# Dividing a group's attention products once, by sums that a column of ones yields, instead of normalising every tile of probabilities

## The reference

```python
q, k, v = split(x @ Wq + bq), split(x @ Wk + bk), split(x @ Wv + bv)
attn = jnp.einsum('bhqd,bhkd->bhqk', q, k) / np.sqrt(8)
attn = jnp.where(causal, attn, -jnp.inf)
attn = jax.nn.softmax(attn, axis=-1)
y = jnp.einsum('bhqk,bhkd->bhqd', attn, v)
y = y.transpose(0, 2, 1, 3).reshape(b, s, e)
return y @ Wo + bo
```

## Time and profile before

| | |
|---|---|
| median of 3 runs | 4177.26 us (4172.37 to 4178.75) |
| the profiled execution | 4182.92 us |
| its span (first to last instruction) | 4181.1 us |
| stage 1 in it | 0 to 682 us |
| busy, whole span: PE, DVE, ACT, POOL | 93%, 79%, 74%, 62% |

### The profile page before, as it was taken

One profiled execution on the slowest core, in us unless ns is written; L12 is line 12 of the kernel. 1 busy time (PEld: TensorE's weight loads), 2 busy tenths in 40 slices (PEclk: granted clock), 3 DMA queues, 4 the chain that ended last, 5 costly groups with the idle time before them and its releaser, 6 DMA issues.

```text
span 4181.1 us, 190344 instructions
## 1 busy us (share of the span) xinstructions
PE 3900.5 (93%) x78816; PEld 3039.7 (73%) x78816; DVE 3305.5 (79%) x5294; ACT 3091.6 (74%) x10376; POOL 2581.2 (62%) x2583
## 2 busy tenths in 40 slices
PE   6888885999998999989999989999899999899998
PEld 3555554888866888848888668888488887588884
DVE  6778874988866888938888668989489886698894
ACT  5877785888865888838888658888488886588883
POOL 4667765766645676627666456766377664566660
PEclk9999998999999999999999999999999999999999
DMA  1000001111111111111111111111111111111110
GB/s 35 2 2 2 2 2 53 47 45 45 46 56 38 45 47 45 44 50 44 49 44 46 58 36 47 44 49 42 53 44 47 47 44 61 35 45 46 47 43 26
DMA packets 100195, 167.40 MB, mean 40 GB/s; under 512 B 26224, under 2 KB 33648, under 8 KB 99056
## 3 DMA queue, kind: packets, MB, share of 16 engines
q1 hardware_dynamic: 99312, 154.89, 12.6%
HBM read 26.13 MB, written 2.10 MB: 7 GB/s over the span
## 4 chain that ended last, share of the span: by engine, by line
PE 69%; issue 9%; POOL 3%; DVE 1%; ACT 0%; DMA 0%; SPq 0%; POOLq 0%; DVEq 0%; ACTq 0%
PE s_bank L1177 13%; PE s_bank L1246 10%; PE s_bank L1259 9%; PE s_bank L1198 8%; PE s_bank L1157 5%; PE s_proj L1222 4%; PE s_proj L1223 4%; PE s_proj L1224 4%; PE s_bank L1209 2%; PE s_bank L1210 2%; PE s_bank L1211 2%; PE s_bank L1167 2%; PE s_bank L1140 1%; POOL s_rotated L802 1%; PE s_bank L1289 1%
## 5 line engine op out<-in xcount | busy, mean ns | idle before, releaser
L802 POOL TENSOR_TENSOR s_rotated<-s_rotated,s_by_sin 128x512 f32<-128x512 f32 x768 | 983.8, 1302 | 227.3 <-DVE s_by_sin L1087 225.2
L811 POOL TENSOR_TENSOR s_probs<-s_probs,s_rden 128x256 f32<-128x256 f32 x768 | 479.7, 641 | 729.8 <-DVE s_rden L1027 729.3
L901 ACT ACTIVATE s_probs<-s_bank,s_neg_max 128x64 f32<-128x64 f32 x3072 | 908.0, 310 | 5.7 <-DVE s_neg_max L1020 5.6
L783 DVE TENSOR_TENSOR s_qk<-s_rotated,s_inv_norm 128x1024 f32<-128x1024 f32 x384 | 743.8, 1937 | 11.5
L1082 DVE TENSOR_TENSOR s_rotated<-s_proj,s_cos 128x1024 f32<-128x1024 f32 x384 | 469.6, 1223 | 241.5 <-ACT s_sq L935 240.9
L901 ACT ACTIVATION_READ_ACCUMULATOR s_probs<-s_bank,s_neg_max 128x1 f32 x3072 | 636.1, 207 | 0.0
L891 ACT ACTIVATE s_probs_t<-s_bank 64x512 f32<-64x512 f32 x384 | 226.8, 591 | 524.8 <-PE s_bank L1157 524.8
L1177 PE MATMUL s_bank<-s_qk 32*32 32x64 f32 x49152 | 581.4, 223 | 26.3 <-issue 25.9
L1177 PEld LDWEIGHTS s_bank<-s_qk 32*32 32x32 f32 x49152 | 510.9, 103 | 115.4 <-issue 114.6
L213 POOL TENSOR_TENSOR s_probs<-s_probs,s_rden 128x384 f32<-128x384 f32 (+3 forms) x512 | 406.4, 802 | 206.1 <-DVE s_rden L406 202.2
L824 POOL TENSOR_TENSOR s_sq<-s_sq 128x512 f32<-128x512 f32 x384 | 490.2, 1277 | 65.5 <-ACT s_sq L935 59.8
(11 more groups left out here) (118 smaller groups left out, 8156.2 us busy)
## 6 DMA issues: line engine op xcount, KB each, us to landing
s_v<-s_v SPq DMA_DIRECT2D x384, 192.0 KB, 2.5
s_v<-s_v SPq DMA_DIRECT2D x384, 64.0 KB, 2.4
s_qk<-f_wqk SPq DMA_DIRECT2D x6, 1024.0 KB, 6.4
s_xs_raw<-u SPq DMA_DIRECT2D x48, 128.0 KB
s_xf<-u SPq DMA_DIRECT2D x48, 128.0 KB, 2.3
s_xs_raw<-u SPq DMA_DIRECT2D x48, 127.8 KB
s_xf<-u SPq DMA_DIRECT2D x48, 127.8 KB, 2.6
s_qk<-f_wv SPq DMA_DIRECT2D x6, 512.0 KB, 6.8
```

The source lines that it names most:

```text
L783: return nc.vector.tensor_tensor(qk[:, quad % 2, :, :, at:at + TOKS], rotated[:, par, :, :, :], by, ALU.mult)
L802: nc.gpsimd.tensor_tensor(rotated[:, par, :, half, :], rotated[:, par, :, half, :], by_sin[:, :, 1 - half, :], (ALU.subtract, ALU.add)[half])\
L811: nc.gpsimd.tensor_tensor(part, part, by, ALU.mult).then_inc(S["probs_done"], 1)
L901: last = nc.scalar.activation(probs[:, par, h, b, :], score_bank[h][:, b * KEYS:(b + 1) * KEYS], ACT.Exp, scale=-1.0, bias=neg_max[:, par, ...
```

## The change

The probabilities are no longer normalised. The padded value matrix gets a bias of one in the ninth of each head's 32 columns, where weight and bias were zero; the product of a head's unnormalised probabilities with its values then holds the row sum in that row. When a group's four query blocks are done, ACT copies `y_bank` to `y_t` as before; a new product with a constant matrix `den_row` spreads each head's sum over its 32 partitions, back into `y_bank`; DVE takes the reciprocal of the whole bank (128 x 512) into `inv_den`; and POOL multiplies `y_t` by it. The per-unit reciprocal, the accumulator read and the per-unit multiplication on POOL are gone. The copy stands where it stood (+7), the new product is issued by PE at +8, the reciprocal by DVE at +9, the multiplication by POOL at +10. The next group's first value products (at +10) wait for the reciprocal in place of the copy, the output projection waits for the multiplication. The work at fixed unit numbers moves by three units. One constant more is loaded at the start.

```diff
-WO_AT, RES_LN_AT, X_LN_AT, PREP_AT = 9, 12, 18, 24
+WO_AT, RES_LN_AT, X_LN_AT, PREP_AT = 12, 15, 21, 27
+COPY_LAG, SPREAD_LAG, INVERT_LAG, DIVIDE_LAG = PV_LAG + 1, PV_LAG + 2, PV_LAG + 3, PV_LAG + 4
...
-                 (ident[:, :], d["c_ident"]), (causal[:, :], d["c_causal"]), (own_rows[:, :], d["c_own_rows"])]
+                 (ident[:, :], d["c_ident"]), (causal[:, :], d["c_causal"]), (own_rows[:, :], d["c_own_rows"]),
+                 (den_row[:, :], d["c_den_row"])]
...
+        def group(s, par, t, lag, first):
+            of = behind(s, par, t, lag, first)
+            return (of[0], of[2] // (QB * HPG)) if of and (of[2] + 1) % (QB * HPG) == 0 else None
...
-            def normalise(s, u):
-                n = P * (UNIT_LIST[u][1] + 1)
-                pool.wait_ge(S["rden_done"], s * UNITS + (u + 1))
-                row = probs[:, u % N_PROBS, 0:n]
-                nc.gpsimd.tensor_tensor(row, row, rden[:, u:u + 1].to_broadcast([P, n]), ALU.mult)\
-                  .then_inc(S["probs_done"], 1)
+            def divide(s, g):
+                pool.wait_ge(S["y_inv"], s * GROUPS + (g + 1))
+                nc.gpsimd.tensor_tensor(y_t[:, g, :], y_t[:, g, :], inv_den[:, :], ALU.mult).then_inc(S["y_done"], 1)
...
-                                         bias=neg_max[:, t:t + 1], accum_out=den[:, t:t + 1]).then_inc(S["exp_done"], 1)
+                                         bias=neg_max[:, t:t + 1]).then_inc(S["exp_done"], 1)
...
-                of = behind(s, par, t, 1, first)
+                of = group(s, par, t, INVERT_LAG, first)
                 if of:
-                    u = of[2]
-                    dve.wait_ge(S["exp_done"], of[0] * UNITS + (u + 1))
-                    nc.vector.reciprocal(rden[:, u:u + 1], den[:, u:u + 1]).then_inc(S["rden_done"], 1)
+                    n = of[0] * GROUPS + of[1]
+                    dve.wait_ge(S["y_spread"], n + 1)
+                    wait(dve, S["y_done"], n)
+                    nc.vector.reciprocal(inv_den[:, :], y_bank[:, :]).then_inc(S["y_inv"], 1)
...
             def output(s):
-                pe.wait_ge(S["y_ready"], s * GROUPS + GROUPS)
+                pe.wait_ge(S["y_done"], s * GROUPS + GROUPS)
...
-                    pe.wait_ge(S["probs_done"], us * UNITS + (u + 1))
+                    pe.wait_ge(S["exp_done"], us * UNITS + (u + 1))
...
                     if b == 0 and not (first and g == 0):
-                        pe.wait_ge(S["y_ready"], us * GROUPS + g)
+                        pe.wait_ge(S["y_inv"], us * GROUPS + g)
...
+                of = group(s, par, t, SPREAD_LAG, first)
+                if of:
+                    pe.wait_ge(S["y_ready"], of[0] * GROUPS + of[1] + 1)
+                    nc.tensor.matmul(y_bank[:, :], den_row[:, :], y_t[:, of[1], :], start=True, stop=True)\
+                      .then_inc(S["y_spread"], 1)
...
+        "c_den_row": ((np.arange(P)[:, None] % PADH == HD1)
+                      & (np.arange(P)[:, None] // PADH == np.arange(P)[None, :] // PADH)).astype(f32),
...
+    bv = pad_heads(i["L0_attn_bv"]).reshape(HEADS, PADH)
+    bv[:, HD1] = 1.0
```

More of the change, by code:

```diff
@@ L127, in build_stage1 @@
         neg_max = sb("s1_neg_max", [P, UNITS])
-        den = sb("s1_den", [P, UNITS])
-        rden = sb("s1_rden", [P, UNITS])
+        den_row = sb("s1_den_row", [P, P])
+        inv_den = sb("s1_inv_den", [P, SEQ])
         probs = sb("s1_probs", [P, N_PROBS, SEQ])
@@ L135, in build_stage1 @@
                  "q_split k_ready k_split "
-                 "v_ready diag_vector diag_pool score_done max_done exp_done rden_done probs_done tr_done pt_vector pt_scalar "
-                 "pv_done y_ready wo_done res_done").split()
+                 "v_ready diag_vector diag_pool score_done max_done exp_done tr_done pt_vector pt_scalar "
+                 "pv_done y_ready y_spread y_inv y_done wo_done res_done").split()
         S = {n: sem("s1_" + n) for n in names}
@@ L227, in unit @@
             def unit(s, par, t, first, last):
-                if t < UNITS:
-                    normalise(s, t)
+                of = group(s, par, t, DIVIDE_LAG, first)
+                if of:
+                    divide(*of)
                 if t < UNITS and not last:
@@ L295, in unit @@
                     nc.scalar.activation(probs[:, t % N_PROBS, 0:n], score_bank[t % 4][:, 0:n], ACT.Exp, scale=-1.0,
-                                         bias=neg_max[:, t:t + 1], accum_out=den[:, t:t + 1]).then_inc(S["exp_done"], 1)
[L297 to L301, removed]
+                                         bias=neg_max[:, t:t + 1]).then_inc(S["exp_done"], 1)
+                of = group(s, par, t, COPY_LAG, first)
+                if of:
+                    g = of[1]
+                    act.wait_ge(S["pv_done"], of[0] * SETS + (g + 1) * QB)
                     if g == 0 and not first:
@@ L1393, in lay_out @@
         "a_bk": four_times(np.asarray(i["L0_attn_bk"])[None]).reshape(GROUPS, P).T,
-        "a_bv": pad_heads(i["L0_attn_bv"]), "a_bo": np.asarray(i["L0_attn_bo"])[:, None],
+        "a_bv": bv.reshape(HEADS * PADH), "a_bo": np.asarray(i["L0_attn_bo"])[:, None],
         "f_wqk": qk_all.reshape(DEPTH, DIM, QUADS * 4 * P),
```

## The result

The changed kernel takes 4328.16 us (median of 4 runs, 4322.53 to 4332.34) against 4174.82 us: 1.0367 times the time before, 95% interval 1.0349 to 1.0385. It is slower, outside the range that was given, and 160 us above the forecast.

What follows compares the result with a forecast made beforehand. No engine full, four waiting for each other: 12.6 us of old waits against 11.0 us of new work and waits, 80.2 to 78.6 us a sequence; eight save 12.8, less 3.4 at the ends: 4168 us, range 4122 to 4224 (own 4145 to 4190).

Steps and rivals of the forecast that it cites:

- The reciprocal of 128x512 at 0.69 us: DVE's new reciprocal, four a sequence: 512 elements at 1.05 ns each, 2.4 us of DVE a sequence.
- second rival: DVE's reciprocal is slow and PE waits for the excess: 4211 us at 2.05 us, 4287 at 4.4; chance 0.20.
- The wait for it: PE's value products at +10 wait for DVE's reciprocal: 0.8 us each, 3.2 us a sequence.
- The old waits that go, 12.6 us: PE's waits at transposes, scores, projections and variance that vanish: 12.6 us a sequence, leaving 0.8 at transposes and scores.
- POOL's leg: Transposes waiting for POOL's normalised probabilities: by itself worth 1.3 to 8.1 us a sequence.
- The knot between DVE and ACT: Per-unit reciprocal stands before later maxima, so DVE can't run ahead of ACT; DVE's 6.1 us wait a sequence goes.
- The product 3.4 us and its wait 4.4 us: Spreading product on PE at +8, 0.86 us each, and its wait for ACT's copy of y, 1.1 us each.
- The wait for the inversion, 3.2 us: PE's value products at +10 wait 0.8 us for DVE's reciprocal; bounds nothing to 1.3 us each.
- The shift at nothing, -1 to +1 us: Fixed-place work moved three units later: no cost, bounds -1 to +1 us a sequence.
- The ends, 3.4 us: Once: one more load, 0.5 us, and the last group's product, reciprocal and POOL division, 2.9 us.
- The query copies near 0.47 us: Sign in the profile after: DVE's query copies, slow ones taken as beside POOL's work, gain 1.8 us a sequence.

Runs made afterwards that it cites:

- filler: Changed kernel with 12 useless bf16 products of 128x512 filling PE's wait for the reciprocal: 4334.30 us, ratio 1.0389.
- no_division: Kernel before without accumulator read, per-unit reciprocal and POOL's multiplication, nothing added or shifted: 4140.12 us, ratio 0.9915.
- shift_only: Kernel before without any division, with output projection, layer norms and projections three units later: 4155.54 us, ratio 0.9940.
- own_bank: Changed kernel with inversion as Exp(-Ln(x)) on ACT and the spreading product in its own bank, taken from the four score banks: 4218.71 us, ratio 1.0108.

## Why the prediction was wrong, by its own steps

- **The reciprocal of 128x512 at 0.69 us: wrong, and the main cause.** It takes 3.35 us. The text had the slow reciprocal as its second rival, with prices of 2.05 and 4.4 us, and chose against it by the equal minima of one and four elements. The minimum of several hundred short instructions is no price; the medians, at 3.7 ns an element, were nearer to the 6.25 ns, and the two prices of the rival, 2.05 and 4.4 us, enclose the 3.35 us. The page that the prediction cites from the Trainium skill ("VectorE: DVE Perf Modes", on the fixed hardware budget) speaks of a repeat count of 8. The runs show 6.25 ns an element, about six times the 1.05 ns of the reduction in the earlier trace rows: fewer than eight, far more than one. The estimate of 4.3 us from that page was nearer than the 0.69 us that was taken. The weight should have gone to the rival.
- **The wait for it: right in kind.** The value products wait 3.2 us, which is what the rival's mechanism says. What the rival lacked is the clock: by its terms 3.35 us is 4 x 2.66 = 10.6 us a sequence, and measured are 99.1 - 85.2 = 13.9. The 3.7 us that filler saved by keeping the clock up are about the difference.
- **The old waits that go, 12.6 us: three times too much.** Measured 4.4 us. The step that failed is the one from "DVE and ACT now lie some 15 us below PE's 74.9" to 0.8 us of waits left at transposes and scores: in no_division the two lie 18 us below the length of the sequence, and PE still waits 28.5 us in five sequences at the transposes alone, 5.7 each. It compared sums over a sequence, where the bound changes every few units.
- **POOL's leg, 1.3 to 8.1 us:** 2.5 us, in its range. The knot between DVE and ACT: 1.9 us.
- **The product 3.4 us and its wait 4.4 us:** the wait is 1.0 us each, nearly as said, but the two together lengthen a sequence by 3.6 us only. This error of 4.2 us went the other way and hid half of the 8.2 us by which the old waits were overestimated.
- **The wait for the inversion, 3.2 us:** 3.3 us, with 0.5 us a group seen at PE and POOL's division in it.
- **The shift at nothing, -1 to +1 us:** +2.5 us. Not in the bounds.
- **The ends, 3.4 us:** the last chain is longer, the reciprocal being 3.35 us, and the output projection behind it runs its first passes at the low clock (its eight passes take 5.70 us there against 3.70 in the earlier trace rows, the granted clock is 0.50 over the first 3.1 us of them). Stage 1 is 156.0 us longer (838.3 against 682.3), of which eight sequences are 151.2, so the ends cost about 4.8 us.
- **The query copies near 0.47 us: right cause, but POOL's other work stayed.** Over 200 to 600 us their mean is 589 ns after and 619 before. All 12 of 48 that take over 0.6 us run beside an instruction of POOL, such as the division that the change itself put there; beside an idle POOL none is slow:

```profile
221.05 1.60 DVE L375 TENSOR_SCALAR s_q_diag<-s_q_split,s_own_rows 128x512 fp32r<-128x512 f32 x1
221.10 1.27 POOL L220 TENSOR_TENSOR s_y<-s_y,s_inv_den 128x512 f32<-128x512 f32 x1 [2.81 <-DVE s_inv_den L414]
...
223.04 0.47 DVE L375 TENSOR_SCALAR s_q_diag<-s_q_split,s_own_rows 128x512 fp32r<-128x512 f32 x1
```

In terms of a sequence: -4.4 (division out), +2.5 (shift), +3.6 (product and its wait), +3.3 (inversion at 0.68 us, and division), +13.9 (the reciprocal's excess) make +18.9 us, which is 99.1 - 80.2. With the reciprocal as forecast it would still be +5.0 where -1.6 was predicted: 8.2 us too much for the old waits and 2.5 us for the shift, less the 4.2 us of the product's wait.

## What to carry to other kernels

Price an operation at two sizes, and as near as possible to the width it will have, before it is made hundreds of times wider; here sixty-four reciprocals of 158 ns became four of 3347 ns, more time in all, in a place where PE and ACT wait for them. A result that another engine uses in the very next step of a shared loop can be dear: with one step more of distance (and other work moved as well) a sequence was 8.2 us shorter here. And a gain that is summed from mean loads over a loop body should be checked stretch by stretch: here 12.6 us were summed and 4.4 us came, most likely because different engines bound different stretches.

## What the runs showed of the hardware that was not expected

- DVE's reciprocal of float32 costs about 6.25 ns an element (202 ns at 8 elements a partition, 1753 at 256, 3353 at 512, all from SBUF, and 3347 at 512 from PSUM); a copy of 512 elements takes 427 ns from SBUF and 681 from PSUM.
- PE's granted clock fell to 0.53 for about 3.6 us after it had stood idle for 3.3 us, and stayed at 1.00 where useless products filled the wait; that shortened a sequence by 3.7 us, products included. Waits of 1.8 us (shift_only, filler) and 2.7 us (own_bank) were followed by a clock of 0.50 as well.
- A copy of 128x512 on DVE that takes 0.47 us alone took up to 1.60 us beside an instruction of POOL.
- The unchanged stage 2 took 3482 us and 3525 us in two kernels that differ in stage 1 only; why is open.
